# Output projection: loading w1 in eight parts, two behind each of four groups, instead of in one transfer

## What is computed

```
x = x + g_msa * (attention(modulate(layernorm(x), sh_msa, sc_msa)) @ W_out + b_out)
x = x + g_mlp * (gelu(modulate(layernorm(x), sh_mlp, sc_mlp) @ W1 + b1) @ W2 + b2)
```

## Time and profile before

| | us |
|---|---|
| median of 3 runs | 3096.3 (3093.09 to 3096.42) |
| the profiled execution, its own time | 3096.48 |
| its span | 3094.6 |
| PE busy | 3023.7 (98%) |
| DVE busy | 1827.9 (59%) |
| ACT busy | 1367.0 (44%) |
| POOL busy | 803.9 (26%) |
| mean granted TensorE clock | 0.99 |

### The profile page before, as it was taken

The page is one execution under the profiler, slowest core; times in us unless marked ns, Lnnn a source line. Parts: engine busy times, 40 slices in busy tenths (PEclk is TensorE's granted clock), DMA queues, the critical chain, the costliest instruction groups (busy, mean ns, idle before and its releaser), DMA issues.

```text
span 3094.6 us, 61621 instructions
## 1 busy us (share of the span) xinstructions
PE 3023.7 (98%) x24578; PEld 2406.8 (78%) x24578; DVE 1827.9 (59%) x2694; ACT 1367.0 (44%) x2840; POOL 803.9 (26%) x523
## 2 busy tenths in 40 slices
PE   8799999999999899999999999999999999999998
PEld 5689997888888677777777777777778888878887
DVE  4378981222112688888888888888556433333432
ACT  2256662222222577777777777777222211111111
POOL 1001112000000343344443444446445101111110
PEclk9899999999999999999999999999999999999999
DMA  5643323333333343333333333332564001010100
GB/s 185 231 170 116 113 67 116 109 122 105 108 106 109 95 115 93 98 83 85 94 88 97 94 83 87 94 90 84 202 247 143 28 1 35 28 35 28 35 14 14
DMA packets 197425, 297.59 MB, mean 96 GB/s; under 512 B 27768, under 2 KB 105752, under 8 KB 194616
## 3 DMA queue, kind: packets, MB, share of 16 engines
q1 hardware_dynamic: 187304, 284.93, 29.3%
q0 software_dynamic: 576, 6.29, 0.6%
q10 hardware_dynamic: 9296, 2.77, 0.4%
HBM read 190.44 MB, written 103.49 MB: 95 GB/s over the span
## 4 chain that ended last, share of the span: by engine, by line
PE 63%; DMA 2%; DVE 1%; ACT 0%; issue 0%; POOL 0%; SPq 0%; DVEq 0%; ACTq 0%; POOLq 0%
PE b_po L1369 15%; PE b_ps L1340 12%; PE d_pf L1842 11%; PE d_po L1853 11%; PE b_tp_act L1352 7%; PE c_po L1615 3%; PE b_tp_dve L1352 3%; DMA c_ot<-o_t 2%; DVE c_ol L1631 0%; PE d_pt L1834 0%; DVE o_first_rest L1631 0%; ACT b_p L1308 0%; POOL d_y L1783 0%; DVE norm_st L865 0%; SPq L1208 0%
## 5 line engine op out<-in xcount | busy, mean ns | idle before, releaser
L1399 DVE TENSOR_REDUCE b_nm<-b_ps 128x1 f32<-128x1024 f32 x512 | 602.1, 1217 | 17.9 <-PE b_ps L1340 4.8
L1308 ACT ACTIVATE b_p<-b_ps,b_nm 128x1024 f32<-128x1024 f32 x512 | 564.6, 1112 | 29.5 <-DVE b_nm L1399 29.5
L1369 PE MATMUL b_po<-b_pt,b_v 128*64 128x256 f32 x4096 | 498.3, 385 | 0.8 <-DVE b_pt L1419 0.8
L1313 ACT ACTIVATE b_pt<-b_tp_act 128x512 f32<-128x512 f32 x512 | 307.9, 601 | 305.6 <-PE b_tp_dve L1352 305.6
L1419 DVE COPY b_pt<-b_tp_dve 128x512 f32<-128x512 f32 x512 | 351.6, 687 | 117.3 <-PE b_tp_dve L1352 117.2
L1352 PEld LDWEIGHTS b_tp_act<-ident,b_p 64*128 64x128 f32 x4096 | 311.7, 138 | 117.6 <-issue 100.7
L1369 PEld LDWEIGHTS b_po<-b_pt,b_v 128*64 128x64 f32 x4096 | 272.1, 136 | 128.5 <-ACT b_pt L1313 0.9
L1352 PE MATMUL b_tp_act<-ident,b_p 64*128 64x64 f32 x4096 | 347.8, 225 | 2.4 <-issue 2.4
L1352 PE MATMUL b_tp_dve<-ident,b_p 64*128 64x64 f32 x4096 | 348.2, 225 | 0.0
L1817 ACT ACTIVATE d_ge<-d_pf,b_t 128x512 f32<-128x512 f32 x128 | 88.2, 689 | 579.7 <-PE d_pf L1842 579.7
L1352 PEld LDWEIGHTS b_tp_dve<-ident,b_p 64*128 64x128 f32 x4096 | 312.0, 138 | 15.2
(11 more groups left out here) (283 smaller groups left out, 6109.0 us busy)
## 6 DMA issues: line engine op xcount, KB each, us to landing
b_raw_q<-q_t SPq DMA_DIRECT2D x124, 256.0 KB, 4.2
q_t<-p_qk SPq DMA_DIRECT2D x64, 256.0 KB, 2.0
k_t<-p_qk SPq DMA_DIRECT2D x64, 256.0 KB, 2.0
v_n<-p_vs SPq DMA_DIRECT2D x32, 512.0 KB, 3.2
b_v<-v_n SPq DMA_DIRECT2D x32, 512.0 KB, 3.9
b_raw_k<-k_t SPq DMA_DIRECT2D x124, 128.0 KB, 4.3
c_ot<-o_t SPq DMA_DIRECT2D x7, 2048.0 KB, 7.9
a_x<-x SPq DMA_DIRECT2D x32, 256.0 KB, 3.4
```

Of the source, the lines that this page charges most:

```text
L1308: act.activation(pr[k % 4][:], ps[k % 2][:], ACT.Exp, bias=nm[:, k % 4:k % 4 + 1], accum_out=rs[:, n:n + 1]).then_inc(exp_done, 1)
L1313: act.activation(dst, src, ACT.Copy).then_inc(t_out[0], 1)
L1369: mm = pe.matmul(po[rows, (blk % 2) * 2 * P:(blk % 2 + 1) * 2 * P], vt[u][:, kc, rows], pt[blk % 2][h][:, kc, :], start=(kc == 0), stop=(k ...
L1399: dve.tensor_reduce(nm[:, k % 4:k % 4 + 1], ps[k % 2][:], axis=AX.X, op=ALU.max, negate=True).then_inc(max_done, 1)
```

## The change

The one transfer of 4 MB in group 1 is replaced by eight of 512 KB, two in each of groups 1 to 4, at the same place of the group: after the load of y (and of gate and bias rows, if there are any). ACT's wait counts all eight.

```diff
--- before.py
+++ after.py
@@ -1536,8 +1536,9 @@
                         load_y(g + 2)
                     if hf and b + 2 < B:
                         load_gate(b + 2)
-                    if g == 1:
-                        sp.dma_start(w1_raw[:], t["w1"].rearrange("(k p) n -> p k n", p=P)).then_inc(w1_in, 16)
+                    if 1 <= g <= NW // 2:
+                        for n in (2 * g - 2, 2 * g - 1):
+                            sp.dma_start(w1_part(w1_raw, n), w1_part(t["w1"].rearrange("(k p) n -> p k n", p=P), n)).then_inc(w1_in, 16)
                 else:
                     for n in range(GT):
                         sp.wait_ge(y_done, g * GT + n + 1)
@@ -1590,7 +1591,7 @@
                 for n in range(GT):
                     if T_AT[n] // GT == g:
                         modulate(n)
-            act.wait_ge(w1_in, 16)
+            act.wait_ge(w1_in, 16 * NW)
             act.wait_ge(m_done, (NG - 1) * GT)
             for n in range(NW):
                 act.copy(w1_part(w1h, n), w1_part(w1_raw, n)).then_inc(w1_rounded, 1)
```

## The result

| | before | after |
|---|---|---|
| median of 7 runs each | 3096.42 us | 3085.68 us (3084.73 to 3086.80) |
| ratio, 95% interval | | 0.9965 (0.9953 to 0.9976) |
| span of the profiled execution | 3094.6 us | 3082.9 us |
| from the output projection's first matmul to the MLP's first | 186.4 us | 177.1 us |

The change takes 10.7 us off; 8.6 were forecast. The ratio's interval, 7 to 15 us, has the forecast inside.

The account below looks back on a forecast made before the run. PE, busy 98% of the span, was taken as the bound; 8.93 us of wait and restart at r = 14 less 0.35 left gave 8.6, other costs 0: 3096.3 - 8.6 = 3087.7 us, range 3085.2 to 3091.3.

Parts of the forecast that it names:

- The largest term: Output projection, r = 14: PE's 7.30 us wait for its transposes and the slow restart nearly vanish, gaining 8.6 us.
- The cause: Group 1's queue: w1's 4 MB, issued 1.6 us ahead of group 4's c_ot load, make that load late, 20.48 us under way.
- Part 1: Ahead of group 4's load: 9.75 us of queue removed, 2.6 us added for two parts, 0.15 us of wait left.
- the forecast's own best case: At r = 14: a pair of parts costs 2.4 us, no wait is left, and the gain is 8.9 us.
- rival 4: At r = 14: 1 to 3 us of wait remain, from slower half rows or another chain step; 3089 to 3091, chance 0.07.
- The restart: PE after the wait at r = 14: 1.63 us of slow matmuls at the lower clock, within 8.93 us in all.
- Part 2: Loads for groups 5, 6 and 7: each 2.6 us further back behind two parts, absorbed by slack; cost 0.
- Parts 3 and 4: SP's three more issues fit into its gaps, and w1's last parts are issued 32 us before ACT reads w1; cost 0.
- 1 (latencies add up): Ahead of group 4's load: parts served one after the other, 3.9 us each; gain 3.3 us, 3093.0, chance 0.07.
- 2 (not w1): Group 4's load delayed by y, gate and bias rows instead of w1; time stays at 3096, chance 0.04.
- 3 (later groups become the late ones): Loads for groups 5 to 7 become late and PE waits 17.2 us longer in all; 3113.5, chance 0.04.
- The signs named ahead: New profile: c_ot landing 13.3 us, clock 1.00, group 5 at 2290.3, parts 1.3 us apart, ACT's idle ended by PE.

Follow-up runs that it names:

- 3: Kernel before, with w1 still one 4 MB transfer but issued in group 2 instead of group 1; 3086.07 us, ratio 0.9972.
- 4: The change, with its w1 parts two in each of groups 2 to 5 instead of 1 to 4; 3087.81 us, ratio 0.9973.
- experiment 5: Kernel before, with w1 whole moved to group 4 and a copy of w1 to a spare HBM tensor behind it; 3091.26 us, ratio 0.9984.
- 11: Kernel before, with w1 whole in group 2 and transposes at blocks (8, 11, 13, 15) instead of (8, 10, 12, 14); 3085.78 us, ratio 0.9963.
- 6: The change, with transposes at blocks (8, 11, 13, 15) instead of (8, 10, 12, 14); 3084.42 us, ratio 0.9966.
- 7: The change run once more, nothing edited; 3085.03 us, ratio 0.9968.
- 9: The change, with PE computing output projection blocks r = 29 and 30 twice; 3094.59 us, ratio 0.9994.
- experiment 12: The change with transposes at (8, 11, 13, 15) and PE's loop over the MLP's middle samples written out; 3081.26 us, ratio 0.9955.
- 2: The change, with four w1 parts in group 1 and four in group 2 instead of two in each of four groups; 3088.53 us, ratio 0.9977.
- 8: The kernel before run once more for its profile, nothing edited; 3096.93 us, ratio 1.0006.
- experiment 10: Kernel before, with PE computing output projection block r = 29 twice; 3098.33 us, ratio 1.0005.
- experiment 1: The change, with all eight w1 parts in group 1, ahead of group 4's load; 3098.17 us, ratio 1.0004.

## Why the prediction was right, point by point

**How right.** 10.7 us were measured where 8.6 were forecast. The largest term, the removal of the wait at r = 14, was right in its mechanism; 2.1 us of the gain came from terms that were too small or missing. The measured 3085.68 us lie 0.5 us above the range's lower end of 3085.2, which was set by the scatter of runs and not by any of these terms, so that it lies inside at all is in part luck.

**The cause** (the load of group 4 behind w1): right, shown from four sides. The landings line up with the bytes ahead:

| w1 ahead of group 4's load | landing | kernels |
|---|---|---|
| nothing | 12.2 to 12.4 us | 3, 4, 5, 11 |
| 1 MB, two parts | 15.1 to 15.9 us | the change, 6, 7, 9, 12 |
| 2 MB, four parts | 17.7 us | 2 |
| 4 MB, one transfer | 23.3 to 23.5 us | before, 8, 10 |
| 4 MB, eight parts | 23.9 us | 1 |

**Part 1, the price of the queue: mis-sized, on both sides.** I took 9.75 us for w1 whole and 2.6 us for a pair; the table gives 23.5 - 12.3 = 11.2 us and 15.4 - 12.3 = 3.1 us. The 430 GB/s were the peak of a window in w1's middle; the price that the load behind it paid is 4.19 MB / 11.2 us = 374 GB/s, and the windows from 2238 to 2254 show 382 GB/s for all traffic together. The net relief was 8.4 us in the first profile (23.5 - 15.1), not 7.15. So `c_ot` was not 0.15 us too late but in time: ACT finished modulate(2) at 2259.97, PE asked at 2260.46. That is the forecast's own best case, 8.9 us instead of 8.6. From the landing to modulate(2)'s end it took about 10.5 us instead of 9.8 (9.92 to PE's transposes), by a step that rival 4 named: DVE's eight splits took 5.55 instead of 4.91 us, and POOL's adds ran until 2250.97, 0.8 us into them. It ate over half a microsecond of slack.

**The restart: mis-sized for most executions.** I measured wait and restart as 8.93 us in one profile. Over one block more (to the third eight matmuls, 5.93 us at r = 8), the two profiles of the kernel before give 8.9 and 10.1 us, experiment 10 gives 9.1 and experiment 1 10.3. So the one profile that I had was at the low end of the four.

**What I had not counted: the loop's turn.** The clock fell there in the three profiles with the long wait and a gap at the turn (before, 1 and 8) and in none of the eight with a gap but no long wait (after, 2 to 7, 11). From the MLP's first matmul on, the first group took 730.5 to 730.8 us and the second 728.4 to 729.9, about 1.5 us apart. 9.5 us at r = 14 (the mean of 8.9 and 10.1) and 1.5 us here make 11.0, against 10.7 measured. The length of the gap doesn't tell them apart: it was 2.49, 2.36 and 1.88 us where the clock fell, and up to 2.63 us where it didn't. Nor does a slow restart in the stage by itself: experiments 4 and 5 had one (3.60 and 3.53 us for eight matmuls) and no fall at the turn. Why the long wait and the fall go together stays open: the wait may decide it, or the time at which the turn comes (2730.7 to 2733.3 us against 2719.8 to 2726.5). Experiments 9 and 10 were to tell it and lost the gap instead.

**Part 2, the later groups:** right in sum, cost 0. The loads came 1.0 to 3.0 us later where I had 2.6, and for group 6 the load did end ACT's wait, where I had said that PE would. I had read the cover of 2.8 us from group 7 and taken group 6 for the same pattern. The rows of before give group 6 only 1.9 us (2299.10 - 2289.52 - 7.7), SP first and then ACT:

```profile
2289.52 0.38 SPq L1494 DMA_DIRECT2D c_ot<-o_t  x1
```

```profile
2299.10 4.27 ACT L1576 CAST o_first_high<-c_ot 128x512 fp32r<-128x512 f32 x8 [17.49 <-PE c_po L1615]
```

A load 3.0 us later is thus 1.1 us late for ACT, as measured, and DVE's slack behind it took that. Experiments 3 and 5 show how much cover there was: group 5's load could come 7.3 us later for nothing, and group 7's 19 us before PE stood still.

**Parts 3 and 4** (SP's issues, w1's use): right; the two issues took 1.43 us, where I had 0.96, and still ended before the split that lets `c_ot` go.

**The rivals.** 1 (latencies add up): fallen; four parts cost 5.4 us, 1.35 each, and eight at once cost 11.6 us. The Trainium skill's fit, "DMA: Bandwidth & Descriptors", section "Anatomy of one DMA", made for transfers issued from GpSimd, gives for eight transfers if they are summed an estimate of 8 x 3.2 = 25.6 us. The 11.6 us of experiment 1 disagree with that sum: in transfers issued together from SP the fixed part overlaps for the most part. 2 (not w1): fallen by experiments 3 and 4. 3 (later groups become the late ones): its mechanism is real and was forced in experiment 5, by 8 MB ahead of group 7's load; the change's 1 MB doesn't do it. 4 was right on DVE's splits, and the slack took it; half rows of 4 KB did not go clearly slower (11.6 us for eight parts against 11.2 for one transfer, with SP's eight issues in the 11.6).

**The signs named ahead.** Group 4's load was to land 13.3 us after its issue and took 12.0; group 5's first matmul was to come at 2290.3 and came at 2288.16, 1.4 us of that because the whole stage began earlier; the pair of parts in group 1 landed 1.2 us apart, where 1.3 was named; the granted clock was 1.00 from 2262 to 2276, as named. Only the sign on ACT's idle time failed, at group 6.

## What to carry to other kernels

A large prefetch delays whatever is issued behind it in the queue: here 11.2 us for 4 MB, 3.1 us for 1 MB. Ask not how to make it smaller but which load behind it has slack: one group later, the same 4 MB in one piece cost nothing. Read that slack through all engines between the load and the bound one, and expect more than the timeline of an early load shows, since work that runs late can run alone (DVE's eight splits in 4.91 us instead of 11.49).

## What the runs showed of the hardware that I had not expected

- PE stands still for 1.8 to 2.6 us at the jump back of its loop, waiting for no data, and the gap vanishes with the jump (experiment 12) or with 48 or 96 PE instructions more ahead of the loop (10 and 9), together with the 16 KB packet of the instruction queue. The Trainium skill, "Runtime: NRT & Kernel Launch", section "Instruction fetch mechanics", says that code is fetched in blocks and that a taken branch out of the blocks at hand has to wait for a fetch. The trace agrees: the packet lies at the gap wherever there is one (2728.02 in the kernel before), and is missing where there is none.
- A short wait may or may not bring the clock down: PE waited 2.09 us in experiment 4 and 1.88 us at the turn in experiment 1, and the granted clock then was 0.50, the lower level, but after 2.36 us at the turn in experiments 3 and 11, and after 2.63 us in 6, it stayed at 1.00.
- The same load with the same queue ahead varies: group 3's `c_ot` took 10.7 to 12.6 us to land over the profiles, and moved PE's wait at r = 10 between 0.5 and 2.1 us. In the six above 11.2 us SP's own issue of it took 1.4 to 1.8 us instead of 0.51 (in two below, too, 1.3 and 1.4). It may explain part of the spread of the runs. In the three profiles with the later transposes (6, 11 and 12) PE doesn't feel it.
